# All four batches of the shared experts ahead of the routed loop, and scatters that wait for TensorE's steps

## The reference, cut to what matters

```python
    for i in range(sh_gate.shape[0]):                       # 2 shared experts, F = 352
        shared = shared + _swiglu(x, sh_gate[i], sh_up[i], sh_down[i])
    w, sel = jax.lax.top_k(probs, K)                        # K = 2 of E = 8
    for e in range(exp_gate.shape[0]):
        routed = routed + Wte[:, e:e + 1] * _swiglu(x, exp_gate[e], exp_up[e], exp_down[e])
    out = shared + SCALE * routed
```

## Time and profile before

| | |
|---|---|
| timed, median of 3 runs | 404.04 us (400.24 to 404.82) |
| profiled execution, span | 423.3 us |
| TensorE busy | 371.6 us, 88% |
| VectorE, ScalarE, GpSimd busy | 255.6, 181.4, 150.8 us |
| DMA | 46.54 MB, mean 110 GB/s |
| mean granted TensorE clock | 0.941 |

### The profile page before, as it was taken

How to read it: one execution, slowest core, us unless ns; L and a number is a source line. 1 busy time by engine, 2 the same in 40 slices (tenths; PEclk the granted TensorE clock), 3 DMA queues, 4 the chain that set the end, 5 groups by cost and what they waited for, 6 DMA issues and landing times.

```text
span 423.3 us, 8003 instructions
## 1 busy us (share of the span) xinstructions
PE 371.6 (88%) x2614; PEld 224.7 (53%) x2615; DVE 255.6 (60%) x566; ACT 181.4 (43%) x314; POOL 150.8 (36%) x128
## 2 busy tenths in 40 slices
PE   7789399999999999892325999999999999999993
PEld 2334254455454454460102466777777777775661
DVE  3996979998666637640113535565565565555475
ACT  5258426758466664430113413333333333332460
POOL 2646405543525520076770000223322223322444
PEclk9969889999999999997556999999999999999997
DMA  7925413663664500022221002232223222221952
GB/s 239 379 64 218 159 40 107 206 192 105 206 192 129 185 0 2 0 102 100 87 100 37 2 12 53 64 99 75 75 75 89 84 76 75 75 59 42 312 185 99
DMA packets 31894, 46.54 MB, mean 110 GB/s; under 512 B 9249, under 2 KB 23585, under 8 KB 31745
## 3 DMA queue, kind: packets, MB, share of 16 engines
q1 hardware_dynamic: 28464, 36.94, 28.8%
q0 software_dynamic: 3408, 9.33, 6.3%
HBM read 29.70 MB, written 16.55 MB: 109 GB/s over the span
## 4 chain that ended last, share of the span: by engine, by line
PE 62%; DVE 15%; another core or an unknown queue 8%; ACT 5%; DMA 4%; issue 3%; POOL 0%; SPq 0%; POOLq 0%; ACTq 0%; DVEq 0%
PE bank L986 52%; PE bank L1214 3%; PE bank L1128 2%; PE bank L1198 2%; DVE wacc L674 2%; DMA w1s<-results 2%; DVE prod L897 2%; DVE wacc L654 2%; DMA x<-wc 1%; DMA results<-yb,ids 1%; DVE x L885 1%; PE bank L1042 1%; ACT sil L585 1%; ACT acts L595 1%
## 5 line engine op out<-in xcount | busy, mean ns | idle before, releaser
L986 PE MATMUL bank<-hs,w1s 128*128 128x512 f16 x264 | 64.6, 400 | 26.7 <-issue 17.4
L986 PE MATMUL bank<-w0s,hs 128*128 128x512 f16 x384 | 87.6, 383 | 0.1
L458 POOL DMA_INDIRECT results<-yb,ids x39 | 37.4, 959 | 130.5 <-ACT yb L619 117.4
L986 PE MATMUL bank<-w1s,rT 128*128 x468 | 76.2, 313 | 1.5 <-DVE rT L950 1.5
L437 POOL TENSOR_TENSOR w1s<-piece,w1s 128x1360 f16<-128x1360 f32 x16 | 44.6, 2797 | 66.8 <-ACT piece L546 66.8
L810 DVE SCALAR_TENSOR_TENSOR x<-bank,coef,x 128x256 f32<-128x256 f32 x128 | 54.8, 477 | 19.0 <-PE bank L986 18.6
L986 PEld LDWEIGHTS bank<-w0s,hs 128*128 128x128 f16 x384 | 37.5, 99 | 43.3 <-issue 1.6
L986 PEld LDWEIGHTS bank<-hs,w1s 128*128 128x128 f16 x264 | 25.9, 102 | 61.6 <-issue 25.6
L986 PEld LDWEIGHTS bank<-w1s,rT 128*128 128x128 f16 x468 | 44.0, 98 | 22.0 <-issue 2.0
L986 PE MATMUL bank<-w1s,aT 128*128 (+1 forms) x351 | 44.8, 272 | 0.8 <-DVE aT L943 0.8
L613 ACT ACTIVATE ract<-prod 128x352 f16<-128x352 f32 x39 | 19.4, 497 | 58.4 <-DVE prod L956 57.4
(11 more groups left out here) (141 smaller groups left out, 463.6 us busy)
## 6 DMA issues: line engine op xcount, KB each, us to landing
piece<-w SPq DMA_DIRECT2D x16, 680.0 KB, 4.6
rows<-slot_rows SPq DMA_DIRECT2D x39, 128.5 KB, 2.1
slot_rows<-zrow SPq DMA_DIRECT2D x11, 385.5 KB, 6.0
w1s<-results SPq DMA_DIRECT2D x6, 512.0 KB, 8.3
x<-wc SPq DMA_DIRECT2D x4, 512.0 KB, 6.5
w1s<-xT SPq DMA_DIRECT2D x4, 512.0 KB, 7.0
w1s<-w SPq DMA_DIRECT2D x4, 512.0 KB, 9.7
x<-x SPq DMA_DIRECT2D x1, 2048.0 KB, 9.3
```

Of the source, the lines that this page charges most:

```text
L458: pool.indirect_dma_start(results, bass.IndirectOffsetOnAxis(ids[:, q:q + 1], 0), yb[:, q], None).then_inc(s_put[q], 16)
L986: mm = nc.tensor.matmul(out_ap, l, r, start=(i == 0), stop=(i == len(terms) - 1))
```

## The change

All 24 units and all four down projections stand ahead of the loop: down of batch 0 behind unit 7 as before, batch 1 behind unit 13, batch 2 behind unit 19, batch 3 behind unit 23, which is the last. The down projections are no longer split or interleaved. ScalarE's and VectorE's parts follow the same order, and behind the loop they have only the scaling and the combines. The scatters of token rows each get two more waits: the n-th waits for the n-th pair of a list (`spaced`) that goes over units 7 to 23, one entry for each unit and one for each quarter of the four down projections; the first waits for 8 units, the 32nd for 24 units and 15 quarters.

```diff
-    EARLY = 3 * ST
-    DOWN = {ST + 1: 0, EARLY - 1: 1, EARLY + 1: 2}
+    UNITS = B * ST
+    DOWN = {ST + 1: 0, 2 * ST + 1: 1, 3 * ST + 1: 2, UNITS - 1: 3}
...
-            return (i + i // EARLY) % 2
+            return i % 2
...
+            spaced, quarters = [], 0
+            for i in range(ST + 1, UNITS):
+                spaced.append((i + 1, quarters))
+                for q in range(TPB if i in DOWN else 0):
+                    quarters += 1
+                    spaced.append((i + 1, quarters))
+
             pool.wait_ge(sm["s_zero"], 16 * (NP - 2))
             pool.wait_ge(sm["s_idx"], 1)
             for k in range(K_TOP):
...
+                    units, quarters = spaced[k * NT + t]
+                    pool.wait_ge(sm["s_gu"], units)
+                    if quarters:
+                        pool.wait_ge(sm["s_dn"], quarters)
                     pool.indirect_dma_start(slot_rows, bass.IndirectOffsetOnAxis(idx[:, k, t:t + 1], 0),
                                             xrow[:, t], None).then_inc(sm["s_scat"], 16)
...
-            for i in range(EARLY, B * ST):
-                shared_act(i)
-                for c in SCALED.get(i, ()):
-                    act.wait_ge(s_yg[c], 16 * K_TOP)
-                    act.wait_ge(sm["s_w1"], 1)
-                    for t in range(c * TPB, (c + 1) * TPB):
-                        y = yg[c][:, 0, t % TPB]
-                        nc.scalar.activation(y, y, ACT.Copy, scale=W1[:, t:t + 1]).then_inc(sm["s_scaled"], 1)
+            act.wait_ge(sm["s_w1"], 1)
+            for c in range(B):
+                act.wait_ge(s_yg[c], 16 * K_TOP)
+                for t in range(c * TPB, (c + 1) * TPB):
+                    y = yg[c][:, 0, t % TPB]
+                    nc.scalar.activation(y, y, ACT.Copy, scale=W1[:, t:t + 1]).then_inc(sm["s_scaled"], 1)
...
-            t = 0
-            for i in range(EARLY, B * ST):
-                shared_dve(i)
-                if i in DOWN:
-                    accumulate(DOWN[i], range(TPB))
-                    t = TPB
-                elif TPB <= t < 2 * TPB:
-                    combine(t)
-                    combine(t + 1)
-                    t += 2
-            for t in range(t, NT):
+            for t in range(NT):
                 combine(t)
-            accumulate(B - 1)
...
+            def down(c):
+
+                pe.wait_ge(sm["s_alo"], (c + 1) * ST)
...
-            pe.wait_ge(sm["s_acc"], TPB + 1)
+            pe.wait_ge(sm["s_acc"], NT - TPB + 1)
             for s in range(-2, 3):
...
-                if s == TILES - 2:
-                    gate_up(EARLY)
-
-            pe.wait_ge(sm["s_rcx"], TILES)
-
-            for i in range(EARLY, B * ST):
-                if i > EARLY:
-                    if i == EARLY + 1:
-                        pe.wait_ge(sm["s_rprod"], TILES)
-                    gate_up(i)
-                if i in DOWN:
-                    pe.wait_ge(sm["s_ry"], TILES)
-                    down(DOWN[i])
-            down(B - 1, (range(ST - 2), range(ST - 2, ST)))
```

More of the change, by code:

```diff
@@ L69, in build_program @@
     SR = [P] * (ST - 1) + [REST]
-    EARLY = 3 * ST
-    DOWN = {ST + 1: 0, EARLY - 1: 1, EARLY + 1: 2}
+    UNITS = B * ST
+    DOWN = {ST + 1: 0, 2 * ST + 1: 1, 3 * ST + 1: 2, UNITS - 1: 3}
     WARM = 9
-    SCALED = {EARLY + 1: (0, 1), EARLY + 3: (2,), B * ST - 1: (3,)}
     G2 = G - 2
@@ L462, in _ @@
                 c, q = t // TPB, t % TPB
-                if t % TPB == 0 and c != B - 1:
+                if t % TPB == 0:
                     pool.wait_ge(sm["s_acc"], (c + 1) * TPB)
@@ L595, in shared_act @@
                 nc.scalar.activation(acts[0:M, c % 2, f, HI], prod[0:M, p], ACT.Copy).then_inc(sm["s_ahi"], 1)
-            for i in range(EARLY):
+            for i in range(UNITS):
                 shared_act(i)
@@ L619, in step @@
                     nc.scalar.activation(yb[:, q], bank[6 + q][:, 0:D], ACT.Copy).then_inc(sm["s_ry"], 1)
-            act.wait_ge(sm["s_prod"], EARLY)
+            act.wait_ge(sm["s_prod"], UNITS)
             run_tiles(act, step, 1)
             act.wait_ge(sm["s_rprod"], TILES)
-            for i in range(EARLY, B * ST):
-                shared_act(i)
-                for c in SCALED.get(i, ()):
-                    act.wait_ge(s_yg[c], 16 * K_TOP)
-                    act.wait_ge(sm["s_w1"], 1)
-                    for t in range(c * TPB, (c + 1) * TPB):
-                        y = yg[c][:, 0, t % TPB]
-                        nc.scalar.activation(y, y, ACT.Copy, scale=W1[:, t:t + 1]).then_inc(sm["s_scaled"], 1)
+            act.wait_ge(sm["s_w1"], 1)
[4 more added lines that the diff above has]
+                    nc.scalar.activation(y, y, ACT.Copy, scale=W1[:, t:t + 1]).then_inc(sm["s_scaled"], 1)
         @block.vector
@@ L903, in shared_dve, with accumulate @@
                                         ALU.subtract).then_inc(sm["s_alo"], 1)
-            def accumulate(c, tiles=()):
-                if c == B - 1:
-                    dve.wait_ge(sm["s_cmb"], NT)
+            def accumulate(c):
                 for q in range(TPB):
@@ L913, in accumulate @@
                                                    ALU.mult, ALU.add).then_inc(sm["s_acc"], 1)
-                    if tiles:
-                        combine(tiles[q])
             tr_lo(TWO - 1)
-            for i in range(EARLY):
+            for i in range(UNITS):
                 shared_dve(i)
@@ L960, in step @@
                                             ALU.subtract).then_inc(sm["s_rlo"], 1)
-            dve.wait_ge(sm["s_ahi"], EARLY)
+            dve.wait_ge(sm["s_ahi"], UNITS)
             run_tiles(dve, step, 2)
             shares1()
-            t = 0
-            for i in range(EARLY, B * ST):
-                shared_dve(i)
-                if i in DOWN:
-                    accumulate(DOWN[i], range(TPB))
-                    t = TPB
-                elif TPB <= t < 2 * TPB:
-                    combine(t)
-                    combine(t + 1)
-                    t += 2
-            for t in range(t, NT):
+            for t in range(NT):
                 combine(t)
-            accumulate(B - 1)
         @block.tensor
@@ L1113, in _ @@
                             token_rows(c, (2, 3))
[L1115 to L1132, removed]
+            def down(c):
+                pe.wait_ge(sm["s_alo"], (c + 1) * ST)
+                for q in range(TPB):
+                    if c == 0:
+                        pe.wait_ge(sm["s_rows"], NT)
+                        pe.wait_ge(sm["s_idx"], 1)
+                    else:
+                        pe.wait_ge(sm["s_acc"], (c - 1) * TPB + q + 1)
+                    for f in range(ST):
+                        for n, (a, b) in enumerate(PASSES):
+                            mm = nc.tensor.matmul(bank[4 + q][:, 0:D],
+                                                  acts[0:SR[f], c % 2, f, a, q * P:(q + 1) * P], w_dn(b, f),
+                                                  start=(f == 0 and n == 0), stop=(f == ST - 1 and n == 2))
+                    mm.then_inc(sm["s_dn"], 1)
             def gate_up(i, between=None):
@@ L1168, in experts @@
                     skip_runtime_bounds_check_because="the table's entries are clamped where it is made")[1]
-            for i in range(EARLY):
-                if i == EARLY - 1:
+            for i in range(UNITS):
+                if i == UNITS - 1:
                     pe.wait_ge(sm["s_idx"], 2)
```

## The result

| | before | changed |
|---|---|---|
| timed, median (us) | 404.06 (400.24 to 404.82, 4 runs) | 425.07 (424.42 to 425.74, 4 runs) |
| profiled execution, span | 423.3 | 422.7 |
| the same execution's own time | - | 424.42 |

The changed kernel takes 1.056 times as long, 95% interval 1.052 to 1.061: 21 us slower. In every run listed here the device time is 1.7 to 1.9 us above the span.

What follows compares the result with a forecast made beforehand. Taken as matmul-bound but for a stall in the traced execution only, with a tail set by transfers and GpSimd's adds: span 423.3 + 6.0 - 10.0 = 419.3, plus 2 for timed terms, gives 421 us, range 411 to 430.

Steps and rivals of the forecast that it cites:

- D: Start of the first down projection behind the ranking; the stage ahead of it is the same program in every kernel.
- The timed runs have no hold: TensorE's late signals beside the 32 token-row scatters, 25.6 us in the profiled execution, are little or nothing in timed runs.
- span less hold: Old program's profiled span without the late-signal stall: 423.3 - 25.6 = 397.7 us, 2.5 under the fastest timed run.
- The wait of 6.2 us ahead of the loop: Old program, no stall: TensorE done at 219.3, last scatter's row landed at 225.5, so 6.2 us idle.
- The 31.4 us: Matmuls moved ahead of the loop, said to fill a 6.2 us wait and a tail with 10 us to give.
- Ahead of the loop, D to T: From the first down projection behind the ranking to the loop's first transposes; loop start forecast at 257.2, +6.0 us.
- a bound of 1.8: Ahead of the loop: +1.8 us for each idle gap behind which TensorE starts at its lower clock, 1.2 GHz.
- Spacing the other 31 costs nothing: Token-row scatters except the last, ahead of the loop: each has 2.2 to 2.6 us where 1.26 suffices.
- The loop, -1.2: In the loop: without unit 18 in its last steps it ends 1.2 us sooner, between 0 and -2.7.
- Behind the loop: The tail, set by transfers and GpSimd's adds, gives back 10.0 us, the loop's 1.2 included.
- +2 to timed terms: From span to timed terms: 2 us added, most of the 2.5 between 397.7 and the fastest timed run.
- A remnant of hold: Ahead of the loop: the timed median's excess beyond the added 2 us may be leftover stall, which spacing would remove.

Runs made afterwards that it cites:

- e1: The kernel before, unchanged, profiled again: 402.31 us, ratio 0.998.
- e2: The changed kernel without the scatters' added waits for units and quarters: 422.62 us, ratio to before 1.053.
- e4: The changed kernel without the scatters' added waits, and with the last down projection in two parts as in the old program: 416.51 us, ratio to before 1.037.
- e8: Against the kernel before, all 24 units and three down projections ahead of the loop, the fourth behind it, no added waits: 411.08 us, ratio 1.026.
- e3: The kernel before with two more units (18 and 19) ahead of the loop: 398.0 us, ratio 0.989.
- e6: The kernel before with four more units (18 to 21) ahead of the loop: 400.42 us, ratio 1.000.
- e5: The kernel before with units 18 to 23 and the last two down projections left out, nothing added ahead: 394.13 us, ratio 0.982.
- e7: Two more units ahead of the loop, plus another order of ScalarE's and VectorE's work behind it, against the kernel before: 396.15 us, ratio 0.988.

## Why the prediction was right

Forecast 421, measured 425.07, inside 411 to 430. In the terms of its span: forecast 178.6 + 78.6 + 138.75 + 23.4 = 419.3, measured 175.2 + 81.6 + 140.1 + 25.8 = 422.7. So the terms were 3.0, 1.3 and 2.4 us too small, and the earlier D took 3.5 of these 6.7 back. That part is luck: with D where it lay before, the span would have been 426 and the time near 428, still inside the range.

- **The timed runs have no hold:** right, and shown by e1. The reading "span less hold" gave 397.7 for the old program; its executions have spans of 396.6 to 403.1.
- **The wait of 6.2 us ahead of the loop:** right; 6.53 measured in e1. The 31.4 us said to have filled it and the tail are 31.6 by the prediction's own steps (five units of 2.59, one of 1.30, two projections of 8.7).
- **Ahead of the loop, D to T:** the mechanism was right, the size short by 3.0 us. The fourth down projection began 67.9 behind D instead of 67.1: a stretch of units behind a down projection takes up to 0.3 us more than its steps (66 matmuls in 14.55 us, where five steps of 2.59 and one of 1.30 make 14.25), and there are three. Behind its wait it ran at the lower clock, 10.34 instead of 8.68 us: the prediction had named this as a bound of 1.8 and left it out of the sum. Its row for it stood behind a stop of 8.58 us; that a stop of 3.5 is enough was first shown by the changed kernel and e2. The last 0.6 lies between the third quarter's matmuls and the last scatter, which started 8.95 behind the projection's start instead of 6.7: from VectorE's taking up the quarter to the scatter's start alone are 0.74 us, where the prediction had 0.2 from the quarter's last matmul. From that scatter to T: 4.8, as read.
- **Spacing the other 31 costs nothing:** right, and there was nothing for it to cure. The waits' price is the last scatter, 3.4 us of D to T, 1.3 to 2.4 timed (e2), where the unhidden wait for unit 23 costs 5.3 with its clock, 6.1 timed (e4).
- **The loop, -1.2:** right where nothing disturbs its start. e4 has 138.7 against 138.75 forecast, and e1 less its late scatter, 141.3, stands 1.2 above the changed kernel, both with a start at the lower clock; the changed kernel has 1.4 more, the first group of matmuls at the lower clock behind the 3.39 us wait (3.41 against 1.96 us), again the bound that was not summed.
- **Behind the loop:** loads to batch 0 5.5 us and to batch 3 14.7 (14.5 forecast), right. GpSimd's 16 adds took 13.5 instead of 12.6 us: the first four step by 0.78, the twelve behind them by 0.87. The other 1.5 us is a wrong anchor. The prediction let the span end 4.0 us behind VectorE's last row, and it ended 5.5 behind it. It ends 6.1 to 6.2 behind GpSimd's last add in all ten traces (417.15 to 423.3 in before, where VectorE's row happened to end 2.1 later). From the forecast's own 408.7 that would have given 414.9 instead of 413.3. e8's expectation made the same mistake, with 1.4 us for the closing additions.
- **+2 to timed terms:** 1.7 to 1.9 in every listed run, but for another reason: this is the fixed distance of time and span, which the prediction did not count when it set spans beside times. Of its 2.5 us between 397.7 and the fastest timed run it is most, and the traced execution of before was about 21.0 us, not 19.3, above the timed median. A remnant of hold was not needed.

On those adds the Trainium skill (SBUF — State Buffer, Who interferes with whom) states that a VectorE instruction with two SBUF inputs contends with a GpSimd instruction that reads SBUF, and calls the ports that they share an exclusive lock. If each held it for its whole length, an add and a combine would take an estimated 0.72 + 0.47 = 1.19 us per tile, by the shortest row of either in the changed kernel. The trace shows 0.87, with rows of 0.90 and 0.94 that overlap: each is slowed, and they don't exclude each other for whole instructions. In e3, where seven combines stepped by 0.47 each, the four adds beside them took 1.40 each.

## What to carry to other kernels

Ahead of moving work, measure the two ends of the move: how long a wait it can fill where it goes (6.5 us here) and what the place it leaves can give (7 us here, not the 31 of its matmuls); the best version found moves just what fits, two units, and takes 0.989 of the time. A profile of one execution can hold a stall that the timed runs don't have: set span less stall against the fastest timed run before curing it. Where two traces are compared, count from an event behind which the programs first differ, and look for the row behind which the end stands equally far in every trace: here it was GpSimd's last add, and not the last row of all.

## What the hardware showed unexpectedly

- One execution of the nine traced with back-to-back scatters showed TensorE's signals up to 15 us late beside 32 scatters issued every 1.26 us; the other eight, beside the same or a fuller TensorE, did not. Its cause is open.
- TensorE's clock behind a stop: stops of 3.0 us (e6), 3.4 (changed), 3.5 (changed, e2), 3.7 (e8), 6.5 (e1) and 7.2 us (e5) were followed by the lower level, with a granted clock of 0.54 to 0.64 in the first 2.5 to 3.5 us of matmuls behind them (72 matmuls in 10.34 and 10.38 instead of 8.75 us, 12 in 3.1 to 3.5 instead of 1.96); two stops close together, of 1.84 and 1.00 us (e3) and of 1.45 and 1.39 (e7), were not (12 in 1.96). Each stop of the first kind costs 1.2 to 1.6 us more than it lasts.
- The stage ahead of D, untouched by any edit, varies by 4.5 us between executions, 2.3 us among four on one chip and 0.9 among four on another.
- The span ends 6.1 to 6.2 us behind GpSimd's last add in all ten traces, whatever VectorE and the stores do behind it.
